# A decoder block's expert rows: scattered by slot, or gathered tile by tile through an inverted token map

## The chip, the cores and the metric

One core of a Trainium2 chip runs the whole program in one launch. The metric is the device time of one execution in microseconds (us), taken as the median of several runs.

## What is computed

The reference is one pre-norm decoder layer on 2048 tokens of width 512, in float32: self attention, cross attention, and a mixture of 16 experts plus a shared one. The last part is what matters here:

```python
scores = softmax(xt @ Wg.T)                      # 2048 x 16
group_scores = scores.reshape(T, 4, 4).max(-1)   # the best 2 of 4 groups stay
topi = top_k(masked, 4)[1]                       # 4 experts of each token
h = silu(einsum('td,eid->eti', xt, W1)) * einsum('td,eid->eti', xt, W3)
y = einsum('etd,te->td', einsum('eti,edi->etd', h, W2), combine)
z = silu(xt @ Ws1.T) * (xt @ Ws3.T) @ Ws2.T      # shared expert, 704 wide
x = x + y + z
```

`xt` is the layer-normed row of each token. The kernel computes an expert only for the tokens that chose it.

## The kernel before

The program runs in stages: self attention, cross attention, then `route_and_share` (layer norm, router, and the first half of the shared expert), `routed_experts`, and `combine_and_share` (the second half of the shared expert, and the sum of each token's four results). Rows are kept as pairs of float16, a high and a low part, so a token's row is 2 x 512 values, 2 KB.

**Slots.** 2048 tokens with 4 experts each give 8192 slots in 64 tiles of 128, and since each expert's slots begin at a new tile, up to `TILES` = 84 tiles exist in DRAM (`slot_rows`, 10752 rows of 2 KB); the number that holds tokens is known only at run time, and the loop over tile pairs stops there. Rows of a tile that belong to no token must hold finite values, so self attention's SP clears all of `slot_rows` with 12 transfers (L773), three in each of four groups.

**Routing.** In `route_and_share`, VectorE (DVE) turns the router's 16 score columns into ranks, choices and, with two products of TensorE (PE) against triangular and full matrices of ones (L1569), into places. L1648 writes `fx_index`: 128 x 64 slot numbers, one for each of the 16 token tiles and 4 choices. Then GpSimd (POOL) issues 64 indirect transfers (L1555), four abreast, each of which writes 128 rows of `fx_rows` from SBUF to their slots in DRAM. Meanwhile DVE computes the weights of the choices (`ro_hit`, L1656 to L1658).

**The shared expert.** `SharedExpert.tensor` is PE's part: four rounds of 512 tokens. `hidden(g)` is 72 products (L78 is the line of the helper) into `sh_ab`, `outputs(g)` 36 products into `sh_yp`. ScalarE (ACT) applies Silu and writes the high part, DVE (for the first three POOL) multiplies and makes the low part (L1453, L1459), and DVE adds the results to `x_sb` (L1464). hidden(0) comes first, then the two products for places; then a loop does hidden(g+1) and outputs(g).

**Routed experts.** SP reads `slot_rows` with transposing transfers into `re_xt` (L1732), two tiles ahead of PE, each as soon as PE has used the buffer. PE does 36 products per tile into `re_ab`, turns the hidden rows (L1809), and does the outputs `re_yp` of a tile behind the hidden products of the next one. POOL keeps the weights: two experts' are in SBUF as pairs; for each further expert e it waits for the last output of expert e-2 (`y_done`), casts the raw weights to the high part (L1765), makes the low part in 16 shares (L1769) and starts the four raw loads of expert e+2 between them (L1749). Results go to `slot_outs` by ACT's queue. Combine gathers them by `fx_index` (L1918).

## Time and profile before

| what | value |
|---|---|
| runs | 1793.79, 1798.22, 1806.79 us; median 1798.22 |
| profiled execution | 1793.67 us, span 1791.9 us |
| TensorE busy | 1477.0 us, 82% of the span |
| mean granted TensorE clock | 0.916 |
| shared expert 0, beside the scatters | about 1042 to 1200 us of the span |
| routed experts | about 1201 to 1678 us |
| combine and shared expert 1 | 1678 us to the end |

Every time in a row of the trace is counted from the span's start; the profiled execution as a whole took 1.8 us more than its span. "Busy" is time in which an engine executes; the releaser behind an arrow is what ended the idle time before a row, and "issue" is idle time for which the profile shows no releaser.

### The profile page before, as it was taken

The page shows a single profiled execution, that of the slowest core. Times are in us where ns is not written, and L with a number is a line of the kernel's source. Part 1 is how long each engine was busy: PE and PEld are TensorE (multiplying, and loading weights), DVE is VectorE, ACT ScalarE, POOL GpSimd, SP SyncE. Part 2 cuts the span into 40 slices and gives each one's busy share as a digit, 9 for nine tenths or more (in the row PEclk, how much of TensorE's full clock was granted, in tenths as well). Part 3 has the DMA queues.
Part 4 walks back from the last instruction along what each step waited for, and adds up shares of the span by engine and source line. Part 5 has one row for each costly group of instructions (what it writes and reads, how often), then busy time and mean ns, then how long its engine had stood idle before and what let it go on. Part 6 is the DMA issues. An engine that isn't in the chain of part 4 may idle for free. (4 is left out here: it accounts for less than half of the span.)

```text
span 1791.9 us, 28528 instructions
## 1 busy us (share of the span) xinstructions
PE 1477.0 (82%) x9520; PEld 694.0 (39%) x9521; DVE 1072.2 (60%) x1851; ACT 621.5 (35%) x1107; POOL 655.4 (37%) x675
## 2 busy tenths in 40 slices
PE   4689999864788888888888595287999999999988
PEld 2355545431222222222222352044555555556443
DVE  6446465567788888888986562022454444444476
ACT  4242404131465665665667540011111111111121
POOL 1000001134633333333201237502664646657374
PEclk9899999895688999999999788598999999999999
DMA  5862538214711311311200125407655566663465
GB/s 210 247 183 89 156 116 237 79 57 87 221 40 35 69 30 42 72 31 30 60 1 1 52 118 205 152 12 157 185 157 162 161 162 150 173 182 87 121 200 186
DMA packets 197159, 211.25 MB, mean 118 GB/s; under 512 B 90000, under 2 KB 162256, under 8 KB 196688
## 3 DMA queue, kind: packets, MB, share of 16 engines
q1 hardware_dynamic: 167696, 123.67, 26.5%
q0 software_dynamic: 18592, 66.99, 12.2%
q10 hardware_dynamic: 10784, 19.47, 2.9%
q8 instruction: 50, 0.82, 0.2%
q14 instruction: 37, 0.30, 0.1%
HBM read 101.09 MB, written 88.87 MB: 106 GB/s over the span
## 5 line engine op out<-in xcount | busy, mean ns | idle before, releaser
L1040 DVE TENSOR_REDUCE ca_mx<-ca_sc 128x1 f32<-128x512 f32 x512 | 327.5, 676 | 81.5 <-PE ca_sc L948 81.0
L78 PE MATMUL re_ab<-fx_w,re_xt 128*128 x1800 | 297.0, 315 | 18.3 <-DMA re_xt<-slot_rows 18.3
L1190 ACT ACTIVATE ca_pt<-ca_st 128x512 f32<-128x512 f32 x512 | 264.7, 596 | 102.7 <-PE ca_st L960 102.7
L948 PE MATMUL ca_sc<-ca_ks,ca_qs 48*128 48x512 f16 x512 | 186.8, 418 | 56.5 <-DVE ca_mx L1040 31.6
L78 PEld LDWEIGHTS re_ab<-fx_w,re_xt 128*128 128x128 f16 x1800 | 173.9, 98 | 116.8 <-issue 21.0
L960 PE MATMUL ca_st<-ca_qs,ca_ks 49*128 49x512 f16 x512 | 171.5, 399 | 42.1 <-ACT ca_pt L1190 36.5
L78 PE MATMUL sh_ab<-fx_xn,sh_pair 128*128 (+3 forms) x576 | 137.6, 398 | 35.5 <-issue 31.7
L78 PE MATMUL re_yp<-fx_w,re_ht 128*128 (+1 forms) x666 | 156.0, 379 | 0.0
L1769 POOL TENSOR_TENSOR fx_w<-re_raw_w,fx_w 128x272 f16<-128x272 f32 x224 | 153.9, 723 | 1.7
L973 PE MATMUL ca_pv<-ca_pt,ca_va 128*32 128x512 f32 x1024 | 149.3, 647 | 1.0 <-DVE ca_turned L1053 0.5
L960 PEld LDWEIGHTS ca_st<-ca_qs,ca_ks 49*128 49x128 f16 x512 | 42.0, 95 | 237.5 <-ACT ca_pt L1190 152.3
L1850 ACT ACTIVATE re_gate<-re_ab 128x352 f32<-128x352 f32 x75 | 34.7, 463 | 255.6 <-PE re_ab L78 197.5
L1765 POOL CAST fx_w<-re_raw_w 128x4352 f16<-128x4352 f32 x14 | 53.3, 3808 | 158.1 <-PE re_yp L78 158.1
L756 POOL TENSOR_TENSOR sa_yt<-sa_yf,sa_yt 128x512 f16<-128x512 f32 x16 | 18.5, 1156 | 250.5 <-ACT sa_yt L690 250.5
L1243 POOL TENSOR_TENSOR ca_tf<-ca_tf,home 128x512 f32<-128x512 f32 x32 | 40.6, 1269 | 176.6 <-DVE ca_rf L1031 176.6
L78 PEld LDWEIGHTS sh_ab<-fx_xn,sh_pair 128*128 128x128 f16 (+1 forms) x576 | 63.1, 110 | 107.3 <-issue 49.1
L1877 DVE TENSOR_TENSOR re_hp<-re_hf,re_hp 128x352 f16<-128x352 f32 x75 | 78.2, 1042 | 42.1 <-ACT re_hp L1852 42.1
L1875 DVE TENSOR_TENSOR re_hf<-re_ab,re_gate 128x352 f32<-128x352 f32 x75 | 39.3, 524 | 105.5 <-PE re_ab L78 105.5
L1886 DVE COPY re_ht<-re_ht_ps 128x768 f16<-128x768 f16 x74 | 41.2, 557 | 101.0 <-PE re_ht_ps L1809 100.9
L1252 POOL TENSOR_TENSOR ca_yt<-ca_yf,ca_yt 128x512 f16<-128x512 f32 x32 | 37.0, 1156 | 170.4 <-ACT ca_yt L1179 170.4
L78 PE MATMUL sa_proj<-sa_xn,sa_w 128*128 128x512 f16 x384 | 89.8, 388 | 5.0 <-DVE home L579 3.9
L1918 POOL DMA_INDIRECT co_yg<-slot_outs,fx_index x64 | 73.4, 1147 | 54.5 <-POOLq L1697 28.6
(242 smaller groups left out, 2343.3 us busy)
## 6 DMA issues: line engine op xcount, KB each, us to landing
re_raw_w<-in_we POOLq DMA_DIRECT2D x56, 544.0 KB, 4.6
slot_rows<-sa_zeros SPq DMA_DIRECT2D x12, 1792.0 KB, 16.0
slot_outs<-re_ys ACTq DMA_DIRECT2D x74, 256.0 KB, 2.0
sa_scratch<-home SPq DMA_DIRECT2D x16, 512.0 KB, 3.7
ca_scratch<-ca_qk SPq DMA_DIRECT2D x64, 128.0 KB, 1.8
sa_qs<-sa_scratch SPq DMA_DIRECT2D x12, 512.0 KB, 6.8
sa_ks<-sa_scratch SPq DMA_DIRECT2D x12, 512.0 KB, 6.6
ca_qs<-ca_scratch SPq DMA_DIRECT2D x48, 128.0 KB, 3.7
```

The costliest lines, as they stand in the source:

```text
L78: last = nc.tensor.matmul(out, lhs(a, c), rhs(b, c), start=(m == 0), stop=(m == total - 1), skip_group_check=parts > 1)
L948: nc.tensor.matmul(sc[:, m % RING, :], qs[rows, c % SLOTS, pair, qt * P:(qt + 1) * P], ks[rows, c % SLOTS, pair, :], start=True, stop=True ...
L960: nc.tensor.matmul(st[:, m % RING, :], ks[rows, b % SLOTS, pair, kt * P:(kt + 1) * P], qs[rows, b % SLOTS, pair, :], start=True, stop=True ...
L973: last = nc.tensor.matmul(pv[j * 32:(j + 1) * 32, :], va[:, b % 2, kt, h, :], pt[:, (4 * qd + j) % 8, :], start=(kt == 0), stop=(kt == 3), ...
L1040: nc.vector.reduce_max(mx[:, qd // 4, qd % 4, 2 * a + jj:2 * a + jj + 1], sc[:, m % RING, :], AX.X).then_inc(maxed, 1)
L1190: nc.scalar.activation(pt[:, (4 * qd + k) % 8, :], st[:, m % RING, :], ACT.Exp, scale=SCALE).then_inc(exp_done, 1)
L1243: nc.gpsimd.tensor_tensor(tf[:, u, :], tf[:, u, :], freq[:, 0, :], ALU.mult).then_inc(rolled, 1)
L1765: nc.gpsimd.tensor_copy(w[:, e % 2, 0, :], raw_w[:, e % 2, :]).then_inc(w_high, 1)
L1769: nc.gpsimd.tensor_tensor(w[:, e % 2, 1, at], raw_w[:, e % 2, at], w[:, e % 2, 0, at], ALU.subtract).then_inc(w_low, 1)
L1877: nc.vector.tensor_tensor(hp[:, s, 1, :], hf[:, s, :], hp[:, s, 0, :], ALU.subtract).then_inc(h_low, 1)
L1886: nc.vector.tensor_copy(ht[:, s, :, :], ht_ps[:, 0:2 * IC, :]).then_inc(ht_ready, 1)
L1918: nc.gpsimd.indirect_dma_start(out=yg[:, m % RING, :], out_offset=None, in_=slot_outs, in_offset=bass.IndirectOffsetOnAxis(ap=route["index ...
```

## The change

The rows are written to DRAM in token order, and each slot tile is gathered from there.

1. `layer_norm`'s SP stores the 16 tiles of token rows in a new DRAM tensor `token_rows`. The 12 clears of `slot_rows` are gone.
2. DVE splits `fx_index` into tile number (`high`) and row in the tile (`low`), and builds, in four chunks of 16 choices, two one-hot matrices in the freed `fx_rows`: `at_tile` (one operation of 128 x 1344 a chunk) and `at_row`, times the token's number (16 operations of 128 x 128 a chunk). Three products and low parts of the shared expert stand between the chunks. The computation of the weights and the adds of the first round come behind it.
3. PE multiplies them, 64 products of 84 columns summed in one bank, behind hidden(1), which is moved ahead of the loop; DVE casts the sum to `fx_tokens`, 128 x 84: which token's row stands in each slot. A slot without a token gets row 0.
4. POOL gathers the first 40 tiles (`AHEAD`) by it into a ring of 6 in SBUF, four in flight; SP stores each to `slot_rows`, two in flight, and transposes tiles 0 and 1 on the way.
5. The other 44 tiles are gathered and stored by POOL among the routed experts (`both`), in groups of 14, 7, 7, 7 and 9, each ahead of POOL's wait for `y_done` of experts 0 to 4. SP's transposes now also wait for `available`.
6. Combine's first four semaphores are those of the gathers.

```diff
 SPARE = TILES - T * TOPK // P
-assert CT * CLEARS * T // G == TILES and SPARE % (T // G) == 0
+assert SPARE % (T // G) == 0
+AHEAD = 40
...
+        @block.sync
+        def _(sp):
+            for t in range(NT):
+                sp.wait_ge(low_ready, t + 1)
+                sp.dma_start(token_rows[t * P:(t + 1) * P, :], pair(t).rearrange("p h d -> p (h d)")
+                             ).then_inc(rows_stored, 16)
...
-                    at = (g * CLEARS + k) * CT * P
-                    zero(slot_rows[at:at + CT * P], zeros[:, :])
                 share = SPARE // NG
...
@@ -1424,9 +1426,12 @@
 
         hidden(0)
         behind_first()
-        with pe.Fori(0, self.ROUNDS - 1) as g:
-            hidden(g + 1)
-            outputs(g)
+        hidden(1)
+        behind_second()
+        outputs(0)
+        with pe.Fori(0, self.ROUNDS - 2) as g:
+            hidden(g + 2)
+            outputs(g + 1)
         outputs(self.ROUNDS - 1)
...
+class Gathers:
...
+    def fetch(self, pool, m):
+        if m >= self.LANES:
+            pool.wait_ge(self.fetched[m % self.LANES], 16 * (m // self.LANES))
+        if m >= self.RING:
+            pool.wait_ge(self.landed[m % 2], 16 * ((m - self.RING) // 2 + 1))
+        self.start(m)
+
+    def start(self, m):
+        self.nc.gpsimd.indirect_dma_start(
+            out=self.staged[:, m % self.RING, :], out_offset=None, in_=self.token_rows,
+            in_offset=bass.IndirectOffsetOnAxis(ap=self.tokens[:, m:m + 1], axis=0)
+        ).then_inc(self.fetched[m % self.LANES], 16)
+    def store(self, engine, m, lanes, first=0):
+        engine.wait_ge(self.fetched[m % self.LANES], 16 * (m // self.LANES + 1))
+        if m >= first + 2:
+            engine.wait_ge(lanes[m % 2], 16 * ((m - first) // 2))
+        engine.dma_start(self.slot_rows[m * P:(m + 1) * P, :], self.staged[:, m % self.RING, :]).then_inc(lanes[m % 2], 16)
+
+    def take_over(self, pool):
+
+        for lane in self.landed:
+            pool.wait_ge(lane, 16 * AHEAD // 2)
+        pool.sem_inc(self.available, AHEAD)
+
+    def both(self, pool, first, count):
+
+        def store(m):
+            self.store(pool, m, self.landed_late, AHEAD)
+            if m >= AHEAD + 2:
+                pool.sem_inc(self.available, 1)
+
+        for m in range(first, count):
+            if m >= first + 3:
+                store(m - 3)
+            pool.wait_ge(self.fetched[m % self.LANES], 16 * (m // self.LANES))
+            if m >= AHEAD + self.RING:
+                pool.wait_ge(self.landed_late[m % 2], 16 * ((m - self.RING - AHEAD) // 2 + 1))
+            self.start(m)
+        for m in range(max(first, count - 3), count):
+            store(m)
+        if count == TILES and first < count:
+            for lane in self.landed_late:
+                pool.wait_ge(lane, 16 * (TILES - AHEAD) // 2)
+            pool.sem_inc(self.available, 2)
+
...
+        at_tile = flat_rows[:, 0:NT * TOPK * TILES].rearrange("p (n k) -> p n k", k=TILES)
+        at_row = flat_rows[:, NT * TOPK * TILES:NT * TOPK * (TILES + P)].rearrange("p (n k) -> p n k", k=P)
...
+            for m in range(AHEAD):
+                gathers.store(sp, m, gathers.landed)
+                if m in (4, 5):
+                    s = m - 4
+                    sp.wait_ge(gathers.landed[s], 16 * 2)
+                    sp.dma_start_transpose(xt[:, s, :, :], gathers.slot_rows[s * P:(s + 1) * P, :]).then_inc(x_loaded[s], 16)
...
-            pool.wait_ge(milestones, ROUTED)
-            for m, (t, k) in enumerate(sends):
-                if m >= ABREAST:
...
+            pool.wait_ge(rows_stored, 16 * NT)
+            pool.wait_ge(milestones, INVERTED)
+            for m in range(AHEAD):
+                gathers.fetch(pool, m)
...
+            def invert():
+
+                share = NT * TOPK // CHUNKS
+                for n in range(NT * TOPK):
+                    if n % share == 0:
+                        pe.wait_ge(milestones, PLACED + n // share + 1)
+                    last = nc.tensor.matmul(tokens_at, at_row[:, n, :], at_tile[:, n, :], start=(n == 0),
+                                            stop=(n == NT * TOPK - 1))
+                last.then_inc(placed, 1)
+
+            shared.tensor(pe, places_and_totals, invert)
...
+            index = route["index"][:, :, :].rearrange("p t k -> p (t k)")
+            link(nc.vector.tensor_scalar(high_i[:, :], index, 7, None, ALU.arith_shift_right))
+            step(nc.vector.tensor_scalar(low_i[:, :], index, P - 1, None, ALU.bitwise_and))
+            link(nc.vector.tensor_copy(high[:, :], high_i[:, :]))
+            step(nc.vector.tensor_copy(low[:, :], low_i[:, :]))
+            dve.wait_ge(rows_stored, 16 * NT)
+            share = NT * TOPK // CHUNKS
+            for c in range(CHUNKS):
+                n0 = c * share
+                nc.vector.tensor_tensor(
+                    at_tile[:, n0:n0 + share, :],
+                    steps[:, 0:TILES].rearrange("p (o k) -> p o k", o=1).to_broadcast([P, share, TILES]),
+                    high[:, n0:n0 + share].rearrange("p (n o) -> p n o", o=1).to_broadcast([P, share, TILES]), ALU.is_equal)
+                for n in range(n0, n0 + share):
+                    last = nc.vector.tensor_scalar(at_row[:, n, :], steps[:, :], low[:, n:n + 1],
+                                                   token[:, n // TOPK:n // TOPK + 1], ALU.is_equal, ALU.mult)
+                last.then_inc(milestones, 1)
+                if c == 0:
+                    shared.wait_low(dve, shared.by_pool - 1)
+                if c < IC:
+                    shared.product(dve, nc.vector, IC + c)
+                    shared.low_part(dve, nc.vector, IC + c)
+            dve.wait_ge(placed, 2)
+            nc.vector.tensor_copy(route["tokens"][:, :], tokens_at).then_inc(milestones, 1)
+            for t in range(4):
+                shared.add(dve, x_sb, t)
+            step(nc.vector.memset(hit[:, :, :], 0.0))
             for k in range(TOPK):
-                if k < IC:
-                    shared.product(dve, nc.vector, IC + k)
                 tk = top[:, :, k:k + 1].to_broadcast([P, NT, E])
...
-            for t in range(4):
-                shared.add(dve, x_sb, t)
...
-            for s in range(2):
-                turn_rows(s, s)
             n = turns(sp)
             with sp.Fori(0, n) as i:
                 for s in range(2):
 
                     sp.wait_ge(ab_done, 2 * i + s + 1)
-                    sp.sem_inc(slot_free, 1)
+                    sp.sem_inc(freed, 1)
+                    sp.wait_ge(gathers.available, 2 * i + s + 3)
+                    sp.sem_inc(freed, 1)
                     turn_rows(s, 2 * i + 2 + s)
...
+            fetched_by = [AHEAD, AHEAD + 14, AHEAD + 21, AHEAD + 28, AHEAD + 35] + [TILES] * (E - 4)
+            gathers.take_over(pool)
...
             for e in range(2, E):
+                gathers.both(pool, fetched_by[e - 2], fetched_by[e - 1])
                 done = pool.value_load(route["ends"][0:1, e - 2:e - 1], min_val=0, max_val=TILES)
                 pool.wait_ge(y_done, done + 2)
-                pool.sem_inc(w_free, 1)
+                pool.sem_inc(freed, 1)
```

What stands on PE between hidden(0) and the loop over the rounds (`sh_ab` are the hidden products, `sh_yp` the outputs). Before:

```order
L78 MATMUL sh_ab<-fx_xn,sh_pair 96x512 x24
L1569 MATMUL ro_spots<-ro_chosen,ro_earlier 128x256
L1569 MATMUL ro_spots<-ro_chosen,ro_every 128x256
L1427 UNCONDITIONAL_BRANCH
L1427 ISA
```

and after the change:

```order
L1647 MATMUL ro_spots<-ro_chosen,ro_earlier 128x256
L1647 MATMUL ro_spots<-ro_chosen,ro_every 128x256
L77 MATMUL sh_ab<-fx_xn,sh_pair 128x512 x48
L77 MATMUL sh_ab<-fx_xn,sh_pair 96x512 x24
L1657 MATMUL ro_spots<-fx_rows 128x84 x64
L77 MATMUL sh_yp<-sh_pair,sh_ht 128x512 x36
L1432 UNCONDITIONAL_BRANCH
```

hidden(1) and outputs(0) have left the loop, and the 64 products of the inversion stand between them.

On POOL, from the scatters to the wait ahead of expert 2's cast. Before:

```order
L1555 DMA slot_rows<-fx_rows,fx_index 10752x1024 x64
L1474 UNCONDITIONAL_BRANCH
L1745 UNCONDITIONAL_BRANCH
L1749 DMA re_raw_w<-in_we 128x1088 x8
L1761 TENSOR_LOAD fx_ends
```

and after (ten further pairs of L1503 and L1494 stand at the dots):

```order
L1494 DMA ga_staged<-token_rows,fx_tokens 128x1024 x40
L1537 UNCONDITIONAL_BRANCH
L1850 UNCONDITIONAL_BRANCH
L1854 DMA re_raw_w<-in_we 128x1088 x8
L1494 DMA ga_staged<-token_rows,fx_tokens 128x1024 x3
L1503 DMA slot_rows<-ga_staged 128x1024
L1494 DMA ga_staged<-token_rows,fx_tokens 128x1024
...
L1503 DMA slot_rows<-ga_staged 128x1024 x3
L1870 TENSOR_LOAD fx_ends
```

Gathers and stores of 14 tiles have come between the raw loads and the wait.

On DVE, behind the index; `sh_hf` and `sh_ht` are the shared expert's product and low part, `ro_hit` the weights' working tile. Before:

```order
L1648 TENSOR_SCALAR fx_index<-ro_top 128x64
L1649 MEMSET ro_hit 128x256
L1453 TENSOR_TENSOR sh_hf<-sh_gate,sh_lin 128x512
L1656 TENSOR_TENSOR ro_hit<-ro_slot,ro_top 128x256
L1657 TENSOR_TENSOR ro_hit<-ro_hit,ro_s 128x256
```

and after (one chunk of four):

```order
L1737 TENSOR_SCALAR fx_index<-ro_top 128x64
L1739 TENSOR_SCALAR ro_high_i<-fx_index 128x64
L1740 TENSOR_SCALAR ro_low_i<-fx_index 128x64
L1741 CAST ro_high<-ro_high_i 128x64
L1742 CAST ro_low<-ro_low_i 128x64
L1747 TENSOR_TENSOR fx_rows<-ro_steps,ro_high 128x1344
L1752 TENSOR_SCALAR fx_rows<-ro_steps,ro_low,ro_token 128x128 x16
L1458 TENSOR_TENSOR sh_hf<-sh_gate,sh_lin 128x512
L1464 TENSOR_TENSOR sh_ht<-sh_hf,sh_ht 128x512
```

A chunk of one-hot rows has come ahead of each product, and the weights have gone behind the chunks.

## Rows read from the trace of the kernel before

**Rows 1.** The page's part 1: busy us, share of the span, instructions.

```profile
PE 1477.0 (82%) x9520; PEld 694.0 (39%) x9521; DVE 1072.2 (60%) x1851; ACT 621.5 (35%) x1107; POOL 655.4 (37%) x675
```

**Rows 2.** The table by windows: start:end, length, each engine's busy time, granted clock, DMA share.

```profile
core 0: us, PE busy (x) PEld busy (x) DVE busy (x) ACT busy (x) POOL busy (x), PEclk, DMA share, GB/s
1068.00:1095.00 27.00, 24.97 (x117) 11.75 (x115) 16.08 (x32) 4.05 (x7) 20.75 (x19) 1.00 0.46 175
1095.00:1158.00 63.00, 17.19 (x35) 4.76 (x32) 1.38 (x2) 1.72 (x3) 43.20 (x45) 0.57 0.50 191
1158.00:1201.00 43.00, 39.45 (x173) 17.53 (x173) 14.93 (x22) 8.45 (x15) 0.00 (x0) 0.95 0.00 0
1250.00:1678.00 428.00, 410.43 (x2713) 246.28 (x2710) 198.54 (x284) 66.89 (x140) 249.97 (x320) 1.00 0.56 153
1678.00:1792.00 114.00, 99.65 (x432) 45.60 (x432) 73.60 (x104) 20.46 (x36) 73.44 (x64) 0.93 0.62 184
```

**Rows 3.** POOL's groups from 1040 us on: count, busy us, mean ns, idle before by releaser.

```profile
L1918 POOL DMA_INDIRECT co_yg<-slot_outs,fx_index x64 | 73.4, 1147 | 54.5 <-POOLq L1697 28.6 <-issue 15.9 <-DVE x_sb L1938 10.1
L1555 POOL DMA_INDIRECT slot_rows<-fx_rows,fx_index x64 | 63.9, 999 | 23.3 <-issue 19.2 <-DVE ro_hit L1649 4.1
```

**Rows 4.** The timeline of PE in the shared stage: start, us, instruction, idle before.

```profile
1085.16 10.09 PE L78 MATMUL sh_ab<-fx_xn,sh_pair 128*128 x46
...
1124.48 0.58 PE L78 MATMUL sh_ab<-fx_xn,sh_pair 128*96 x1 [2.22 <-issue]
```

**Rows 5.** The timeline of PE at full pace, and its first routed products.

```profile
1059.64 15.70 PE L78 MATMUL sh_ab<-fx_xn,sh_pair 128*128 x72
...
1183.83 15.97 PE L78 MATMUL sh_yp<-sh_pair,sh_ht 128*128 128x512 f16 x72
1204.63 8.03 PE L78 MATMUL re_ab<-fx_w,re_xt 128*128 x36 [4.83 <-DMA re_xt<-slot_rows]
```

**Rows 6.** The timelines of SP's queue and of PE at the clears.

```profile
61.14 11.65 SPq L773 DMA_DIRECT2D slot_rows<-sa_zeros  x3
...
68.90 0.60 PE L466 MATMUL sa_sc<-sa_ks,sa_qs 96*128 96x128 f16 x4 [14.32 <-DMA sa_ks<-sa_scratch]
```

**Rows 7.** The timelines of DVE around the index and of PE at the router.

```profile
1066.23 1.32 DVE L1646 MAX8 ro_top<-ro_slot 128x8 f32<-128x16 f32 x16
1067.58 0.20 DVE L1648 TENSOR_SCALAR fx_index<-ro_top 128x64 int32<-128x64 f32 x1
...
1068.26 0.69 DVE L1453 TENSOR_TENSOR sh_hf<-sh_gate,sh_lin 128x512 f32<-128x512 f32 x1
...
1070.23 0.69 DVE L1459 TENSOR_TENSOR sh_ht<-sh_hf,sh_ht 128x512 f16<-128x512 f32 x1
...
1087.26 1.55 DVE L1665 TENSOR_TENSOR ro_passed<-ro_tile_no,ro_ends 1x1344 f32<-1x1344 f32 x1
...
1039.64 1.16 PE L78 MATMUL ro_spots<-ro_wg,fx_xn 128*128 128x16 f16 x36
```

**Rows 8.** The timeline of POOL in the routed experts.

```profile
1211.18 2.18 POOL L1749 DMA_DIRECT2D re_raw_w<-in_we  x4 [59.57 <-PE re_ab L78]
...
1221.45 1.56 POOL L1749 DMA_DIRECT2D re_raw_w<-in_we  x3 [0.22 <-issue]
1248.06 3.81 POOL L1765 CAST fx_w<-re_raw_w 128x4352 f16<-128x4352 f32 x1 [25.05 <-PE re_yp L78]
...
1272.69 3.80 POOL L1765 CAST fx_w<-re_raw_w 128x4352 f16<-128x4352 f32 x1 [6.36 <-PE re_yp L78]
...
1297.31 3.81 POOL L1765 CAST fx_w<-re_raw_w 128x4352 f16<-128x4352 f32 x1 [6.36 <-PE re_yp L78]
...
1388.79 3.81 POOL L1765 CAST fx_w<-re_raw_w 128x4352 f16<-128x4352 f32 x1 [12.22 <-PE re_yp L78]
```

**Rows 9.** The page's DMA issues, and the landing times of re_xt's transposes.

```profile
slot_outs<-re_ys ACTq DMA_DIRECT2D x74, 256.0 KB, 2.0
...
DMA to landing us min/median/max: 3.0/3.3/18.2
```

More of the change, by code:

```diff
@@ L1474, in route_and_share @@
+def route_and_share(nc, split, sems, ident, x_sb, moments, xn, rows, route, wg_dram, we_dram, token_rows, gathers, first_pairs,
+                    xt, x_loaded):
     with ExitStack() as ctx:
@@ L1518, in route_and_share @@
         hit = sb("hit", [P, NT, E], F32)
+        high_i = sb("high_i", [P, NT * TOPK], I32)
+        low_i = sb("low_i", [P, NT * TOPK], I32)
+        high = sb("high", [P, NT * TOPK], F16)
+        low = sb("low", [P, NT * TOPK], F32)
+        steps32 = sb("steps32", [P, P], F32)
+        steps = sb("steps", [P, P], F16)
+        token = sb("token", [P, NT], F32)
         tile_no = sb("tile_no", [1, TILES], F32)
-        passed = sb("passed", [1, TILES, E], F32)
+        end = NT * TOPK * (TILES + P)
+        passed = flat_rows[0:1, end:end + 2 * TILES * E].bitcast(F32).rearrange("o (t e) -> o t e", e=E)
         owner = sb("owner", [1, TILES], F32)
@@ L1545, in _ @@
                                     base=0, pattern=[[1, P]], channel_multiplier=-1).then_inc(made, 1)
-            sends = [(t, k) for t in range(NT) for k in range(TOPK)]
             for n in range(shared.by_pool):
@@ L1907, in combine_and_share @@
         yg = sb("yg", [P, RING, D], F32)
-        fetched = [sem(f"fetched{r}") for r in range(RING)]
-        used, ready, stored = sem("used"), sem("ready"), sem("stored")
+        fetched = gathers.fetched + [sem(f"fetched{r}") for r in range(gathers.LANES, RING)]
+        earlier = [16 * TILES // gathers.LANES] * gathers.LANES + [0] * (RING - gathers.LANES)
+        used, stored = sem("used"), sem("stored")
         fetches = [(t, k) for t in range(NT) for k in range(TOPK)]
```

86 lines of the change are left out of this document (43 added, 43 removed).

## The prediction, made before the changed kernel was run

> **What bounds the kernel now.** First the page: PE is busy for 1477.0 of 1791.9 us, POOL for 655.4 [rows 1], so PE is the engine to follow, and the question is where it isn't busy. The table by windows answers it [rows 2]: in the shared expert's stage PE has 24.97 of 27 us, then only 17.19 of 63, then 39.45 of 43. The stretch of 63 us is the one hole that the change touches directly. What fills it is seen twice. POOL's groups show the 64 scatters, 0.999 us each, 63.9 in all, with 19.2 us of "issue" between them [rows 3]: 1.30 from start to start. They can begin when the index is ready, at 1067.8, and so last until 1151, and the last one's data lands a few us later. The timeline of PE shows that it waits for no semaphore there: 46 matmuls run in 10.09 us up to 1095, then they come one by one, eleven of them, as the one shown, with 2.22 us of "issue" before it [rows 4]. It is over by 1158, as the scatters are. Nothing in the trace names the cause; it is slow instruction supply that begins 27 us into the scatters. At full pace the hidden part of a round is 72 matmuls in 15.70 us, its outputs 36, half of the 15.97 that 72 take: 8.0 [rows 5]. PE ends the stage at 1199.8, and the first routed product runs at 1204.63, at half clock, for which it waited 4.83 us.
>
> **Clears.** The 12 clears go, three of four issued at 61.14 in 11.65 us. One wait of PE for sa_ks ends behind them, 14.32 us [rows 6]; most of it is the load's own path. Between 0 and 3 us; I take -2.
>
> **Tokens.** The index is written at 1067.58 + 0.20. Four small DVE operations on 64 columns (0.20 each) follow: 1068.7. Then four chunks: one comparison over 1344 columns, 1.55 by the row of the same size, and 16 one-hot rows of 128 columns. Such rows are not in the trace: one over 64 columns takes 0.20 and the 16 MAX8 over 8 start 0.08 apart; I take 0.17 (0.10 to 0.25) and a chunk of 1.5 + 2.7 = 4.2, together 16.8. Between the chunks stand three pairs of product and low part, from 1068.26 to 1070.23 + 0.1 apart with ACT's part between: 2.1 each, 6.3. Sum 1091.8. The last 16 matmuls of 84 columns, by the router's 36 of 16 columns in 1.16 with more columns, about 1.6, the cast and semaphores 0.4 [rows 7]: tokens near 1094 (1088 to 1102). PE meanwhile ends the second hidden part, at 1059.64 + 15.70 = 1075.3 [rows 5], and then has only the 64 matmuls until 1093.7; this wait of 18 us is new, and outputs(0) and everything of PE stand behind it.
>
> **PE's shared stage.** What is left is outputs(0), two rounds of hidden and outputs, outputs(3): 8.0 + 15.7 + 8.0 + 15.7 + 16.0 = 63.4, and 3 for a clock that falls to half in the new wait (before, 0.57 was granted in the hole) [rows 2]: 1160, where it was 1199.8. This takes for granted that the slow supply is gone with the scatters; rival A denies it.
>
> **Gathers.** POOL starts 40 from 1094.3. The nearest rows are co_yg's, also 256 KB by an index: 73.4 busy and 15.9 of issue for 64, 1.40 from start to start [rows 3]. But here each tile's bytes cross the DMA engines twice, in and out by SP, so I take 1.6 (1.30, the scatters' pace, to 2.3): 39 x 1.6 + 6 for the landings of gather and store = 1162.7 (1150 to 1190). Routed starts near 1164. Its first two transposes have been done, so the wait of 4.83 before re_ab goes: first product 1164.1, -40.5. POOL's first raw load then comes at 1168.2 (the first tile runs at full clock; before 6.55 behind the first product, now 4.1), and its second batch, which ends at 1221.45 + 1.56 before, at 1180.0, -43.
>
> **In the experts.** Here the gain is partly given back, and this is the term that decides. POOL's next work before was the cast for expert 2, waiting 25.05 us for PE, then 6.36, then 12.2 in each of the following [rows 8]. Cast and low parts and loads of one expert take 24.63 - 6.36 = 18.3. An expert of four tiles lasts 24.6, one of five 30.5, a tile so 6.1. POOL now has gathers and stores ahead of each of the waits: 14, 7, 7, 7 and 9 tiles. One costs a gather, 1.15 + 0.2, and a store, 0.544 by the raw load's row + 0.16, together 2.05; a group ends with a wait of about 0.5 for its last gather, the fifth with 3 for its last stores. So 29.2 + 3 x 14.9 + 21.5 = 95.4. POOL is then never idle: 1180.0 + 95.4 + 5 x 18.3 = 1366.9 for expert 6's weights, with PE waiting for weights from expert 3 on. Expert 5's last outputs follow one tile later, 1373.0, where it was 1388.79: -15.8. Queued behind POOL's waits are the raw loads of the next expert, and behind these the casts; that is in the sum. From there POOL has no extra work, 18.3 against 30.5, and PE sets the end as before. Of some 40 us won, 25 are given back.
>
> The bound of this price from below: the gathers alone at 1.3 to 1.4, the stores hidden, where POOL's sum falls to 60 and PE's own pace sets the end: at best -43. From above: stores with a whole landing of a 256 KB transfer, 2.0 [rows 9], half of it beside POOL's next gather, 3.0 a tile. I take 2.05, nearest to the rows of issue, since three tiles are in flight.
>
> The longest landing of a transpose before is 18.2 against a median of 3.3 [rows 9], beside the eight raw loads; two tiles of PE cover 12.2. The Trainium skill, "DMA: Bandwidth & Descriptors", section "Queues, rings and completion order", says that each DMA engine takes turns between its queues packet by packet. By that rule a transpose's small packets each wait for one large packet of POOL's queue, and its landing grows several times, wherever POOL moves rows; the slow row agrees in sign. If the landings stay under 12.2 the sum stays as it is. At the slow row's 18.2 each tile so hit would cost the excess, 6.0; seven such tiles would bring the 42 us of rival B by another way, and its chance holds this too.
>
> **Other edits.** The 16 stores of token rows lie in the layer norm, on SP, ahead of the routing. Weights and adds moved behind the tokens: the adds are wanted only from outputs(0), which now comes later itself. PE's loop over rounds is a round shorter and starts a round later in both shared experts; the order of the matmuls in the second one stays but for hidden(1) ahead of outputs(0), as before. Combine's semaphores: nothing. The last stage, 99.65 of 114 [rows 2], is untouched.
>
> **Sum.** 1793.7 (the profiled execution) - 15.8 - 2 = 1775.9. The median of the runs, 1798.2, stands 4.5 above that execution, the lowest 0.1; I add 2: 1778.
>
> **Rivals.**
>
> A, the slow supply stays. For it: its cause is unknown, DRAM is written by rows in both kernels, and 80 transfers are under way. Against it: no such phase shows beside clears or the 64 gathers of the last stage. If it comes 27 us into the gathers, at 1121, PE has 36 us of work left, does about 12% of its full pace (by 35 matmuls in 63 us, at 0.22 each) to 1160 and ends at 1195. POOL is free at 1212, and 1212 + 95.4 + 91.5 + 6.1 = 1405: +16.4 - 2, so 1810.
>
> B, the other side: POOL's share in the experts costs 3.0 a tile, because each store waits for the landing two before it while the DMA engines are shared with loads and transposes. 44 x 0.95 = 42 more than the forecast: 1820. It decides from 2.5 us a tile; over 1% slower from 2.9. For it: the DMA engines are 0.56 busy in the experts' stretch as it is [rows 2], and each tile adds 512 KB to read, stage and write. Against it: the lanes leave three tiles in flight.
>
> C, POOL's share is cheap, near 1.4 a tile: PE sets the pace at once, and nearly all of the 43 stays: 1755.
>
> That the change doesn't do what it says, which is to free PE of the hole, is A as well.
>
> **Chances.** Forecast 0.50, A 0.26, B 0.12, C 0.12. A measurement tells about 1%, here 18 us, from no change: faster is under 1780.2, slower above 1816.2. The forecast's own range is 1765 to 1792, so 0.29 of its 0.50 is faster; with C 0.41. A is 0.16 within and 0.10 slower, B 0.10 slower and 0.02 within. Faster 0.41, same 0.39, slower 0.20. The range runs from C to B, 1754 to 1824.
>
> **What would show it.** Right: tokens cast near 1094; PE with no "issue" rows between 1094 and 1160; the fortieth gather near 1157; re_ab first near 1164; POOL without idle time before the casts of experts 3 to 6, PE waiting for POOL there, some 5 us an expert; the cast of expert 7 near 1373. Wrong: "issue" before single matmuls again (A); stores L1503 with a wait for their own lane, or re_ab waiting for DMA in experts 1 to 6 (B); the cast for expert 7 before 1360 (C). A one-hot row above 0.3 us would shift everything by 8 us or more.

## The result, and the profile after the change

| | kernel before | changed kernel |
|---|---|---|
| median of runs | 1799.41 us (1793.79 to 1806.79, 4 runs) | 1845.59 us (1843.13 to 1855.03, 4 runs) |
| ratio | | 1.027, 95% interval 1.0211 to 1.0328 |
| span of the profiled execution | 1791.9 us | 1841.3 us |
| mean granted clock | 0.916 | 0.902 |

The change makes the kernel 2.7% slower. The forecast was 1778 with a range up to 1824; it was wrong in sign and in range.

The page's first part, and the two groups of it that speak of the change (busy, mean ns, idle before), against [rows 1]:

```profile
PE 1482.8 (81%) x9568; PEld 701.2 (38%) x9585; DVE 1077.8 (59%) x1925; ACT 621.8 (34%) x1107; POOL 696.8 (38%) x741
...
L77 PE MATMUL re_ab<-fx_w,fx_xt 128*128 x1800 | 302.6, 319 | 107.1 <-POOLq L1884 74.3
...
L1494 POOL DMA_INDIRECT ga_staged<-token_rows,fx_tokens x84 | 83.0, 988 | 86.9 <-DMA slot_rows<-ga_staged 34.5
```

PE has hardly more work than before, 1482.8 against 1477.0. But the routed experts' hidden products (`re_ab`) now have 107.1 us of idle time in all before them, 74.3 of it until POOL, at L1884, raised `w_ready` for an expert's weights; before, the same products had waited 18.3 us in all, for transposes. The gathers waited 34.5 us for stores to land. The table by windows, against [rows 2]:

```profile
core 0: us, PE busy (x) PEld busy (x) DVE busy (x) ACT busy (x) POOL busy (x), PEclk, DMA share, GB/s
1068.00:1095.00 27.00, 11.20 (x87) 7.04 (x86) 24.70 (x78) 3.83 (x7) 0.00 (x0) 0.73 0.00 1
1095.00:1158.00 63.00, 62.86 (x297) 29.70 (x298) 28.16 (x50) 10.16 (x18) 29.50 (x29) 0.98 0.83 229
1158.00:1201.00 43.00, 14.84 (x83) 8.18 (x82) 5.00 (x9) 1.92 (x4) 12.63 (x15) 0.68 0.70 223
1250.00:1400.00 150.00, 105.30 (x657) 62.02 (x658) 48.13 (x66) 15.83 (x33) 107.58 (x139) 0.85 0.75 206
```

The hole of 63 us is gone: PE has 62.86 of 63 where it had 17.19. In its place PE has 11.20 of 27 ahead of it, 14.84 of 43 behind it, and 105.30 of 150 in the experts. Note the column before the last, the DMA engines' share: 0.83, 0.70 and 0.75 in the last three windows. The timeline of PE in the shared stage:

```profile
1096.01 8.77 PE L77 MATMUL sh_yp<-sh_pair,sh_ht 128*128 128x512 f16 x36
...
1143.72 15.97 PE L77 MATMUL sh_yp<-sh_pair,sh_ht 128*128 128x512 f16 x72
1186.52 7.15 PE L77 MATMUL re_ab<-fx_w,fx_xt 128*128 x36 [26.82 <-issue]
```

PE ends the stage at 1159.7, as the forecast said (1160), and then stands still for 26.82 us. The profile names no releaser there; the code does. The stage ends for all engines together, so PE stays until SP and POOL have started all 40 gathers and stores, and in the next stage POOL raises `w_ready` for the first two experts only behind `take_over`, which waits until the 40 stores have landed. PE's first product needs only tile 0, and SP had started the transposes of tiles 0 and 1 by 1115. No run tries the stage with a smaller `AHEAD` or with the weights released earlier. The timeline of POOL, through the gathers and what comes after:

```profile
1097.39 1.13 POOL L1494 DMA_INDIRECT ga_staged<-token_rows,fx_tokens  x1 [32.79 <-DVE fx_tokens L1761]
...
1177.06 0.95 POOL L1494 DMA_INDIRECT ga_staged<-token_rows,fx_tokens  x1 [1.23 <-DMA slot_rows<-ga_staged]
...
1202.09 2.10 POOL L1854 DMA_DIRECT2D re_raw_w<-in_we  x4 [7.70 <-DMA re_raw_w<-in_we]
1204.49 1.01 POOL L1494 DMA_INDIRECT ga_staged<-token_rows,fx_tokens  x1 [0.30 <-issue]
...
1213.44 0.59 POOL L1503 DMA_DIRECT2D slot_rows<-ga_staged  x1 [5.40 <-DMA ga_staged<-token_rows,fx_tokens]
...
1233.50 0.58 POOL L1503 DMA_DIRECT2D slot_rows<-ga_staged  x1 [2.50 <-DMA slot_rows<-ga_staged]
...
1245.71 0.54 POOL L1503 DMA_DIRECT2D slot_rows<-ga_staged  x1 [2.26 <-DMA slot_rows<-ga_staged]
1246.84 3.81 POOL L1874 CAST fx_w<-re_raw_w 128x4352 f16<-128x4352 f32 x1 [0.59 <-issue]
...
1285.75 3.81 POOL L1874 CAST fx_w<-re_raw_w 128x4352 f16<-128x4352 f32 x1 [0.32 <-issue]
...
1412.63 4.11 POOL L1874 CAST fx_w<-re_raw_w 128x4352 f16<-128x4352 f32 x1 [2.67 <-DMA slot_rows<-ga_staged]
...
1442.21 3.81 POOL L1874 CAST fx_w<-re_raw_w 128x4352 f16<-128x4352 f32 x1 [8.92 <-PE re_yp L77]
```

The 40 gathers take from 1097.39 to 1177.06, 2.04 us from start to start. Then come POOL's 14 later tiles, from the end of its raw loads at 1204.19 to the cast at 1246.84, and so on: the rows show the pattern of gather, wait, store, and the casts of experts 2, 3, 6 and 7. Before, the cast of expert 7 stood at 1388.79 [rows 8]; it stands at 1442.21. That is +53.4, of which 4.0 come back up to the end.

### The profile page after: what moved, and what is told of

Read it like the earlier page. It is cut to its first block and busy times, and to the rows that moved or that the text cites. A ratio compares the mean times of both kernels' runs of the same rounds, so it can differ in the third digit from the quotient of the medians.

```text
span 1841.3 us, 29056 instructions
## 1 busy us (share of the span) xinstructions
PE 1482.8 (81%) x9568; PEld 701.2 (38%) x9585; DVE 1077.8 (59%) x1925; ACT 621.8 (34%) x1107; POOL 696.8 (38%) x741
## 5 line engine op out<-in xcount | busy, mean ns | idle before, releaser
L77 PE MATMUL re_ab<-fx_w,fx_xt 128*128 x1800 | 302.6, 319 | 107.1 <-POOLq L1884 74.3
L77 PEld LDWEIGHTS re_ab<-fx_w,fx_xt 128*128 128x128 f16 x1800 | 175.5, 100 | 210.6 <-issue 114.7
L950 PE MATMUL ca_sc<-ca_ks,ca_qs 48*128 48x512 f16 x512 | 188.0, 422 | 53.2 <-DVE ca_mx L1042 30.5
L77 PE MATMUL sh_ab<-fx_xn,sh_pair 128*128 128x512 f16 (+3 forms) x576 | 129.1, 387 | 3.8 <-PEq L1804 3.3
L1494 POOL DMA_INDIRECT ga_staged<-token_rows,fx_tokens x84 | 83.0, 988 | 86.9 <-DMA slot_rows<-ga_staged 34.5
L1961 ACT ACTIVATE re_hp<-re_hf 128x352 f16<-128x352 f32 x75 | 37.2, 496 | 169.3 <-DVE re_hf L1984 164.7
L77 PEld LDWEIGHTS re_yp<-fx_w,re_ht 128*128 128x128 f16 (+1 forms) x666 | 65.1, 98 | 69.9 <-issue 1.1
```

The source lines that it names most:

```text
L77: last = nc.tensor.matmul(out, lhs(a, c), rhs(b, c), start=(m == 0), stop=(m == total - 1), skip_group_check=parts > 1)
L950: nc.tensor.matmul(sc[:, m % RING, :], qs[rows, c % SLOTS, pair, qt * P:(qt + 1) * P], ks[rows, c % SLOTS, pair, :], start=True, stop=True ...
L1494: self.nc.gpsimd.indirect_dma_start(out=self.staged[:, m % self.RING, :], out_offset=None, in_=self.token_rows, in_offset=bass.IndirectOff ...
```

## The experiments

The profiled executions differ by up to 9 us in where the shared stage's second hidden part begins (1059.6 to 1068.7), whatever the kernel, so a place in that stage is compared with the first scatter or gather of its own execution.

**What makes the hole?** Runs on the kernel before. "Hole" is the stretch in which PE's matmuls come one by one with "issue" before them [rows 4].

`b_plain`:

```diff
-                nc.gpsimd.indirect_dma_start(
-                    out=slot_rows, out_offset=bass.IndirectOffsetOnAxis(ap=route["index"][:, t, k:k + 1], axis=0),
-                    in_=rows[:, t, :, :].rearrange("p h d -> p (h d)"), in_offset=None
-                ).then_inc(sent[m % ABREAST], 16)
+                pool.dma_start(slot_rows[m * P:(m + 1) * P, :], rows[:, t, :, :].rearrange("p h d -> p (h d)")
+                               ).then_inc(sent[m % ABREAST], 16)
```

> The kernel before, with each of its 64 indirect scatters replaced by a plain store of the same 256 KB from SBUF to slot_rows, same engine, same four abreast. It leaves the routing of rows out. Theory S (the slow supply of PE's instructions comes with the indirect writes of rows, whose targets lie scattered in DRAM): the hole goes, PE issues without gaps, the stage ends near 1151 instead of 1199.8, total near 1747. Rival W (any 17 MB written to DRAM at this rate does it): the hole stays, total near 1794. Rival L (it is the code of the loop over rounds): stays too.

Measured: 1731.22, beside 1801.92 for the kernel before on that chip. PE issues without gaps and ends the stage at 1148.8. The same bytes to DRAM do nothing to PE, so W falls. Nor is it a matter of busy DMA engines: their share was 0.89 here from 1082 to 1125 us, beside a PE that has no "issue" at all, and 0.50 in the hole [rows 2]. The total is 16 us below what S gave; 11.6 of these lie in the experts, where five tiles took 29.3 us instead of 30.5 [rows 8], and this is not explained (see the end).

`b_half`:

```diff
-            sends = [(t, k) for t in range(NT) for k in range(TOPK)]
+            sends = [(t, k) for t in range(NT) for k in range(TOPK // 2)]
```

> The kernel before with only the first 32 of the 64 scatters; half of the rows aren't moved. S and W: the single-file matmuls begin about 27 us into the scatters as before and end as the 32nd scatter lands, about 42 us after the first, so the hole is about 17 us long instead of 63 and the total near 1757. L: the hole stays as long as it is, total near 1794.

Measured: 1755.7, as S and W gave. The gaps begin near 1104, 27 us behind the first scatter, and end at 1123, with the scatters. The hole lasts as long as the scatters do.

`b_order`:

```diff
-        with pe.Fori(0, self.ROUNDS - 1) as g:
-            hidden(g + 1)
-            outputs(g)
+        hidden(1)
+        outputs(0)
+        with pe.Fori(0, self.ROUNDS - 2) as g:
+            hidden(g + 2)
+            outputs(g + 1)
```

> The kernel before with only PE's order changed as in the changed kernel: hidden(1) and outputs(0) written out ahead of the loop over rounds. S and W: the hole stays (it begins when the scatters are 27 us old, whatever code runs), total within 8 us of 1794. L: the hole moves or goes, total down by up to 45 us.

Measured: 1802.97, and the hole is there from 1100 to 1163. L falls: the order of PE's code, which the change also alters, has no part in it. A run that was to put 10 to 25 us ahead of the first scatter gave no result.

`b_abreast2`, and the same timed as `b_abreast2_t`, and `b_abreast3`:

```diff
-ABREAST = 4
+ABREAST = 2
```

(With 3, which doesn't divide 64, the last wait also takes each semaphore's own count.)

> The kernel before with two scatters in flight instead of four. S and W, if it is the number in flight that starves the fetch: scatters 2 us or more apart, PE free of gaps, routed stage from about 1068 + 64 x 2 = 1200 on, total near 1792. If it is the writes as such: gaps as long as the scatters last, about 1200, and a total of 1810 to 1830. L: no change of the hole.

> The kernel before with two scatters in flight, timed: the one run of it was 1760.3 against 1801.9. The same again: 1756 to 1764, a ratio near 0.98.

> The kernel before with three scatters in flight. If three are few enough for the instruction supply: scatters 1.3 us apart instead of 1.5, the routed stage starts 12 us earlier than with two, total near 1748. If they aren't: the hole is back, total 1790 to 1800.

Measured: with two in flight 1760.31 in the first run, where no theory had put it (1792, or 1810 to 1830): PE is free of gaps, but the scatters come 1.52 us apart and not the 2 or more expected. In the median of four it is 1768.74, a ratio of 0.985 (0.9793 to 0.9904), above the 1756 to 1764 expected from the first run. With three 1796.41, 0.9985 (0.9941 to 1.0029), and the hole is back. What differs is told by POOL's groups in one line each (count, busy, mean ns, idle before by releaser); two in flight:

```profile
L1555 POOL DMA_INDIRECT slot_rows<-fx_rows,fx_index x64 | 64.1, 1002 | 36.7 <-DMA slot_rows<-fx_rows,fx_index 31.4 <-DVE ro_hit L1649 4.1 <-issue 1.2
```

three in flight:

```profile
L1555 POOL DMA_INDIRECT slot_rows<-fx_rows,fx_index x64 | 64.3, 1004 | 23.2 <-issue 19.2 <-DVE ro_hit L1649 4.1
```

With two, 59 of the scatters were preceded by a wait for a landing, of 0.53 us on average. With three there was none: the 0.3 us of "issue" before each are the same as with four [rows 3]. So three act like four, and what two bring is a wait before nearly each scatter. A new theory (Q below) says: PE's instructions are held back while POOL issues indirect transfers with no pause between.

**What do the later tiles cost the experts?** Three runs on the changed kernel; a fourth asks what the clears cost.

`a_fit`:

```diff
-            fetched_by = [AHEAD, AHEAD + 14, AHEAD + 21, AHEAD + 28, AHEAD + 35] + [TILES] * (E - 4)
+            fetched_by = [AHEAD + n for n in (0, 8, 10, 12, 16, 20, 24, 28, 32, 36, 40, 42, 44, 44, 44)]
```

> The changed kernel with the 44 later tiles in other groups ahead of the same waits of POOL: 8, 2, 2, 4, 4, 4, 4, 4, 4, 4, 2, 2 instead of 14, 7, 7, 7, 9, so that at some 3 us a tile each group fits into the idle time that POOL has ahead of that cast in the kernel before (25, 6, 6, then 12 us). The order is enough for this routing, in which no expert owns more than five tiles. Theory P (POOL's time ahead of the casts is what the experts lose by): no cast is late any more, the experts run at the pace of before from the first routed product at 1186.5 on, total 1186.5 + 587 = 1774 (1766 to 1780). Rival D (the DMA engines' load delays transposes and raw loads wherever it lies): PE keeps waiting for re_xt or for weights, total above 1810.

Measured: 1811.72, beside 1795.01 for the kernel before: 34 less than the changed kernel's median, but 38 more than P gave. It also lies just above the 1810 from which D was to hold. POOL still goes from work to work. The timeline of one group of four, ahead of expert 6's cast:

```profile
1340.47 1.03 POOL L1494 DMA_INDIRECT ga_staged<-token_rows,fx_tokens  x1 [0.30 <-issue]
...
1346.48 0.58 POOL L1503 DMA_DIRECT2D slot_rows<-ga_staged  x1 [2.45 <-DMA ga_staged<-token_rows,fx_tokens]
...
1352.86 0.54 POOL L1503 DMA_DIRECT2D slot_rows<-ga_staged  x1 [2.05 <-DMA slot_rows<-ga_staged]
1353.71 3.81 POOL L1873 CAST fx_w<-re_raw_w 128x4352 f16<-128x4352 f32 x1 [0.31 <-issue]
```

From the first gather to the cast these four tiles take 13.2 us, not 12.2: each group first waits for its first gather (2.45) and at its end for landings (2.05 before the last store), so a small group costs more per tile: one of two tiles took 8.6 us (26.9 from cast to cast, less 18.3). Other groups of four took up to 15.7 us (34.0 from cast to cast, less 18.3). So P's statement that no cast would be late is wrong. Its mechanism fits the waits of PE's `re_ab` all the same: 33.3 us for late weights, where the changed kernel had 74.3, and 5.8 for transposes, where it had 5.7, so what is left of the loss is still POOL's time. D speaks of waits for weights too, and this total doesn't part the two; `a_thin` does more. The version isn't faster than the kernel before.

`a_thin` (the clears are put back so that the tiles hold numbers):

```diff
     def start(self, m):
+        if m >= AHEAD:
+            self.nc.gpsimd.indirect_dma_start(
+                out=self.staged[0:16, m % self.RING, :], out_offset=None, in_=self.token_rows,
+                in_offset=bass.IndirectOffsetOnAxis(ap=self.tokens[0:16, m:m + 1], axis=0)
+            ).then_inc(self.fetched[m % self.LANES], 16)
+            return
...
-        engine.dma_start(self.slot_rows[m * P:(m + 1) * P, :], self.staged[:, m % self.RING, :]).then_inc(lanes[m % 2], 16)
+        n = P if m < AHEAD else 16
+        engine.dma_start(self.slot_rows[m * P:m * P + n, :], self.staged[0:n, m % self.RING, :]).then_inc(lanes[m % 2], 16)
```

> The changed kernel with 16 of 128 rows gathered and stored in each of the 44 later tiles, so that 1/8 of the bytes moves there with the same instructions; most rows of these tiles aren't moved (slot_rows is cleared ahead, as before the change). Theory B (the 3.05 us a tile are the DMA engines' time for 512 KB beside loads and transposes): a tile falls to POOL's issue time, 1.9, the groups from 134 to 84 us, total near 1793. Rival F (it is the fixed latency of landings with two stores in flight): a tile stays at 2.7 or more, total above 1825.

Measured: 1810.03. B gave 1793, F more than 1825. Three of its rows, the second raw loads, and the casts of experts 2 and 3:

```profile
1205.87 2.09 POOL L1866 DMA_DIRECT2D re_raw_w<-in_we  x4 [7.59 <-DMA re_raw_w<-in_we]
...
1239.14 3.81 POOL L1886 CAST fx_w<-re_raw_w 128x4352 f16<-128x4352 f32 x1 [0.66 <-issue]
...
1272.18 3.81 POOL L1886 CAST fx_w<-re_raw_w 128x4352 f16<-128x4352 f32 x1 [0.40 <-PE re_yp L79]
```

From the end of the loads (1207.96) to the cast the 14 tiles take 31.2 us, 2.2 each; the next seven take 33.04 - 18.3 = 14.7, 2.1 each. The changed kernel took 42.7 and 20.6 for the same. All five groups together took 96.6 us, where the changed kernel had 135.3 and the forecast 95.4. What POOL waited for before its later stores shows where the difference lies (total, times, longest); changed kernel, 1204 to 1413 us:

```profile
POOL slot_rows L1503 <- DMA slot_rows<-ga_staged: 36.7, 21, 2.9
...
POOL slot_rows L1503 <- DMA ga_staged<-token_rows,fx_tokens: 10.9, 5, 5.4
```

and `a_thin`, 1204 to 1380 us:

```profile
POOL slot_rows L1515 <- DMA ga_staged<-token_rows,fx_tokens: 7.7, 4, 4.7
...
POOL slot_rows L1515 <- DMA slot_rows<-ga_staged: 6.0, 6, 1.3
```

This is B: with the bytes gone a tile costs nearly what its instructions cost, and the wait for earlier stores falls from 36.7 us to 6.0. A thin tile has 1/8 of the rows as well as of the bytes; no run tells the two apart. The total lies 17 above my number because I had worked it out with 1.9, and because at 2.2 POOL's work still isn't hidden: PE waited 34.4 us for late weights.

`a_lanes`: four semaphores for the stores of SP and four for those of POOL, each store waiting for the fourth before it.

```diff
-    RING, LANES = 6, 4
+    RING, LANES, EARLY, LATE = 6, 4, 4, 4
...
-        if m >= first + 2:
-            engine.wait_ge(lanes[m % 2], 16 * ((m - first) // 2))
+        s = len(lanes)
+        if m >= first + s:
+            engine.wait_ge(lanes[(m - first) % s], 16 * ((m - first) // s))
...
```

> The changed kernel with four stores in flight instead of two, in both places. B: no or little gain, since the engines are full: the shared stage's gathers stay 2.0 us apart, total within 8 us of the changed kernel's 1843. F: the gathers of the shared stage come 1.4 to 1.6 us apart (-18 us) and a tile in the experts costs 2.3 (-30 us), total near 1797.

Measured: 1853.99, 11 above the 1843 of B, which had allowed 8, and 57 above what F gave. The windows of its gathers in the shared stage and of its first later group:

```profile
1105.00:1172.00 67.00, 59.43 (x274) 27.55 (x272) 28.39 (x49) 10.16 (x18) 37.06 (x37) 0.97 0.93 288
1210.00:1240.00 30.00, 23.85 (x148) 14.09 (x149) 7.46 (x13) 3.35 (x7) 18.24 (x24) 0.89 1.08 258
```

and the same two places of the changed kernel:

```profile
1104.00:1178.00 74.00, 55.55 (x256) 25.81 (x254) 27.00 (x47) 10.16 (x18) 34.83 (x35) 0.90 0.89 255
1213.00:1246.00 33.00, 23.63 (x156) 14.13 (x156) 9.20 (x16) 3.84 (x8) 18.57 (x25) 0.98 1.01 278
```

The DMA engines were 0.89 and 1.01 busy with two stores in flight, 0.93 and 1.08 with four (the table's shares can come out a little over 1). The shared stage's gathers came 1.83 us apart instead of 2.04, which is 8 us, so they didn't "stay 2.0 us apart", as B had it, either. In the experts nothing was won: PE waited 61.7 us for weights and 18.1 for transposes, together 79.8, where the changed kernel had 74.3 and 5.7. F falls.

`a_clears` (the wait for the clears is put back too):

```diff
+                for k in range(CLEARS):
+                    at = (g * CLEARS + k) * CT * P
+                    zero(slot_rows[at:at + CT * P], zeros[:, :])
```

> The changed kernel with the 12 clears of slot_rows put back. If their removal was worth something: 2 to 3 us slower than the changed kernel, with the difference in the first 200 us. If they were hidden: the first 200 us equal, total within 1 us (one run can't tell more than that from the total; the windows can).

Measured: 1846.59, 1.0 above the changed kernel's median. From 60 to 100 us, in the changed kernel:

```profile
60.00:100.00 40.00, 30.61 (x176) 16.59 (x180) 18.27 (x36) 7.59 (x10) 4.48 (x4) 0.83 0.29 73
```

and with the clears:

```profile
60.00:100.00 40.00, 30.28 (x174) 16.34 (x178) 18.37 (x35) 7.33 (x10) 4.48 (x4) 0.83 0.68 211
```

The DMA engines do 0.29 or 0.68, PE 30.61 or 30.28: hidden. PE's wait for `sa_ks` ends at 68.86 without the clears and at 69.19 with them; before it was 68.90 [rows 6].

**Back to the hole, and the forecast's sum.**

`a_allthin`: as `a_thin`, but for all 84 tiles.

> The changed kernel with 16 of 128 rows gathered and stored in each of all 84 tiles: 1/8 of the bytes, all instructions; most rows aren't moved. If the bytes' time in the DMA engines is all that the forecast mis-sized, it now comes out: gathers of the shared stage 1.3 to 1.6 us apart, the routed stage from 1164 on, a tile in the experts 2.1, total 1774 to 1790. If something else is missing as well, it stays above 1800.

Measured: 1816.2. Neither: the hole came back, in a kernel that scatters nothing. PE in it, and behind the dots POOL's gathers at the same time:

```profile
1112.58 0.38 PE L79 MATMUL sh_ab<-fx_xn,sh_pair 128*128 x1 [0.72 <-issue]
...
1118.21 0.59 PE L79 MATMUL sh_ab<-fx_xn,sh_pair 128*128 x1 [2.40 <-issue]
...
1123.92 5.79 PE L79 MATMUL sh_ab<-fx_xn,sh_pair 128*128 x12 [0.81 <-issue]
1136.26 3.69 PE L79 MATMUL sh_ab<-fx_xn,sh_pair 128*96 x9 [6.55 <-issue]
...
1114.92 0.84 POOL L1500 DMA_INDIRECT ga_staged<-token_rows,fx_tokens  x1 [0.30 <-issue]
1117.66 0.83 POOL L1500 DMA_INDIRECT ga_staged<-token_rows,fx_tokens  x1 [1.90 <-DMA slot_rows<-ga_staged]
1120.49 0.96 POOL L1500 DMA_INDIRECT ga_staged<-token_rows,fx_tokens  x1 [2.00 <-DMA slot_rows<-ga_staged]
...
1126.78 0.84 POOL L1500 DMA_INDIRECT ga_staged<-token_rows,fx_tokens  x1 [0.30 <-DMA slot_rows<-ga_staged]
```

PE's gaps begin at 1112, after 12 gathers without a wait. At 1117.66 and 1120.49 POOL waits 1.90 and 2.00 us for stores, and from 1120 on PE runs again; in the next 18 gathers, which have no such wait, it stands again (6.55 before 1136.26). S falls with this too: these gathers read, and move 32 KB each. What they have in common with the scatters is POOL's unbroken row of indirect transfers, and its pace, 1.14 us from start to start here. The bytes' part can still be read: 40 gathers took 1098.23 to 1153.39, 1.41 from start to start, against 2.04.

Two more kernels from the kernel before, `b_pause16` and `b_pause8`:

```diff
                 if m >= ABREAST:
                     pool.wait_ge(sent[m % ABREAST], 16 * (m // ABREAST))
+                if m and m % 16 == 0:
+                    pool.wait_ge(sent[(m - 1) % ABREAST], 16 * ((m - 1) // ABREAST + 1))
```

> The kernel before, four scatters in flight, with a wait for the landing of the scatter just issued ahead of every 16th. Theory Q (PE's instruction supply is held back while POOL issues indirect transfers without a pause, and a pause of a few us lets it catch up): no run of scatters is longer than 16, or 20 us, and the hole began after 21 of them, 27 us; no hole or short gaps, scatters done near 1162, total 1745 to 1760. Rival N (it is four in flight, or the writes as such): the hole stays but for the three pauses, total 1780 to 1800.

> The same with the wait ahead of every 8th. Q: no hole at all, seven pauses of some 3 us, scatters done near 1172, total 1755 to 1765. N: gaps between the pauses, total above 1775.

Measured: every 16th 1770.46, ratio 0.9837 (0.9812 to 0.9862); every 8th 1768.6, 0.9825 (0.9792 to 0.9858). The totals decide nothing: the first lies between Q's 1760 and N's 1780, the second above Q's 1765 and below N's 1775. PE's rows do. The sum of what PE waited for from 1090 to 1730 us, by releaser (total, times, longest), in the kernel before:

```profile
PE sh_ab L78 <- issue: 31.7, 16, 5.8
...
PE sh_yp L78 <- issue: 14.9, 8, 2.9
```

with a pause every 16th:

```profile
PE sh_ab L78 <- issue: 10.5, 11, 3.7
PE sh_yp L78 <- issue: 10.3, 6, 3.2
```

and with one every 8th:

```profile
PE re_ab L78 <- DMA re_xt<-slot_rows: 43.1, 4, 38.2
...
PE sh_ab L78 <- issue: 2.7, 4, 1.7
```

Of 46.6 us of "issue" some 20 are left with 16, and 2.7 with 8. So N falls: with four in flight and the same writes, seven pauses of 2.5 us take the hole away. Now PE waits 38.2 us once, for the first transpose, because the scatters end late: the limit has gone to POOL.

Q in its own words doesn't hold, though. With a pause every 16th, PE's first gap is this one, and it begins at 1105, at the ninth scatter behind the first pause, after the first 16 in a row had passed without any:

```profile
1108.26 3.47 PE L78 MATMUL sh_yp<-sh_pair,sh_ht 128*128 128x512 f16 x9 [3.24 <-issue]
```

And in the last stage of the kernel before, POOL issues 24 gathers between 1697.22 and 1730.17 us with 0.3 us before each but the first, while PE has no "issue" in the whole stage and, in this row, its full pace:

```profile
1724.16 15.70 PE L78 MATMUL sh_ab<-fx_xn,sh_pair 128*128 x72
```

Those come 1.43 us apart; in the hole it is 1.27. By the mean from the first to the last transfer, the runs with a hole have 1.31 (kernel before, three in flight), 1.41 (`a_allthin`) and 1.42 (every 16th), those without 1.52 (two in flight), 1.54 (`a_thinpause`, below), 1.58 (every 8th) and 2.04 (changed kernel). So it may be the pace of the indirect transfers and not the missing pause that counts; no run parts the two, for every pause slows the pace as well.

`a_thinpause`: `a_allthin` with such a wait ahead of every 6th gather of the shared stage.

> The changed kernel with 1/8 of the bytes in all 84 tiles, as in the run before, and a wait for the landing of the gather just issued ahead of every 6th in the shared stage. Q: the single-file matmuls that this run had without the pauses go, PE ends the stage near 1160, and what the forecast took for the bytes is all that is left out of it: total 1776 to 1792. N, or something else still missing from the forecast: above 1800.

Measured: 1786.61, in the range that Q gave; the single-file matmuls are gone, and PE has one "issue" of 0.54 us left in the shared stage. This execution's shared stage began 8.5 us later than the changed kernel's (its second hidden part at 1068.71 against 1060.19). PE starts the experts at 1174.77, which is 1166.3 without that lag, against the forecast's 1164.1. The cast of expert 7:

```profile
1389.26 3.81 POOL L1888 CAST fx_w<-re_raw_w 128x4352 f16<-128x4352 f32 x1 [9.02 <-PE re_yp L79]
```

Without the lag it is 1380.8; the forecast had 1373.0, the changed kernel 1442.21.

## Why the prediction was wrong

The term that failed is the price of a later tile in the experts, 2.05 us, which measured 3.07; behind it comes the pace of the first 40 gathers, 1.6 us, which measured 2.04. Both were priced by POOL's instructions, and both are set by the rows that the DMA engines have to move. By its own steps, between the forecast's 1775.9 and the profiled 1843.1:

- **Clears** (-2): measured 0, since they were hidden. 2 us missed.
- **Tokens** (ready near 1094): the gathers began at 1097.4. The chunks were on time but for the one-hot rows, here the first 16:

```profile
1070.13 3.65 DVE L1752 TENSOR_SCALAR fx_rows<-ro_steps,ro_low,ro_token 128x128 f16<-128x128 f16 x16
```

  0.23 each instead of 0.17; the three pairs of product and low part cost 2.0 instead of 2.1. Late by 3.1 in all.
- **PE's shared stage** (1160): the number was right, 1159.7, in part by luck. PE began outputs(0) at 1096.0, 2.3 late, and the 3 us set aside for the clock were nearly all left over: 63.7 us for a sum of 63.4. And the forecast let the hole go "with the scatters". It went beside gathers that came 2.04 us apart, most of which waited for a store to land; where they come faster, rival A comes true, as `a_allthin` shows. At the forecast's own 1.6 no run was made.
- **Gathers** (1.6 us apart, taken from 1.30 to 2.3): measured 2.04, +17.3 over 39; with the later start and a longer landing at the end, the first routed product came at 1186.5 instead of 1164.1, +22.4. The reason was in the text, that the bytes cross twice, but only 0.2 us of it in the number. `a_allthin` gives 1.41 with 1/8 of the bytes.
- **In the experts** (2.05 a tile, 95.4 in all): the step that failed most. The five groups took 42.7, 20.6, 19.3, 21.6 and 31.1, together 135.3, or 3.07 a tile: +39.9. The forecast priced POOL's instructions, took them as nearest to the rows, and had the DMA engines' load, 0.56 [rows 2], only in rival B. `a_thin` shows that the instructions' price was right (96.6 us in all, 2.2 a tile) and that nearly 1 us a tile is the wait for the bytes; `a_lanes` that it isn't the number of stores in flight.
- The rest up to expert 7's cast was 7 us longer than the fixed 15.9, 18.3 and 6.1 of the sum, and from there on 4.0 were won that had not been forecast. 22.4 + 39.9 + 6.9 - 4.0 + 2.0 = 67.2, which is the whole difference.

Of the rivals, B had the mechanism (stores waiting for landings, on shared DMA engines) and its price, 3.0, within 0.1; of its two reasons the shared engines hold, and the wait for "the landing two before it" doesn't, by `a_lanes`. Its 1820 lacked the 22.4 us of the shared stage, 17.3 of which have the same cause. It was given 0.12. The range went wrong there too: its upper end, 1824, took the dear tiles and the slow gathers one at a time, though one cause drives both. The rule that was weighed, from the Trainium skill's page "DMA: Bandwidth & Descriptors", section "Queues, rings and completion order", that queues are served in turn packet by packet, would have the transposes fall behind beside POOL's rows. PE waited 5.7 us for them in all, against 18.3 before, so it cost nothing here that the runs show; but PE stood waiting for weights at the time, and a slower transpose could hide behind that. The changed kernel's profile gives no landing time for its transposes.

The sign follows: PE ends the shared stage 40.1 us earlier and waits 12.6 less for transposes, and it pays for that with 26.8 us of waiting for the gathers at the stage's end and 74.3 of waiting for weights. That leaves 48.4 us of the 49.4 by which the span grew. The end of the hole can be had for less: with two scatters in flight, or a pause every 16th or every 8th, and nothing else of the change, the kernel before runs at 0.985, 0.9837 and 0.9825 of its time. These three are the fastest versions of this study that do the whole computation. Their intervals overlap, so none of them is shown to be the best; each excludes 1, so each beats the kernel before, by under 2%.

## What to carry to other kernels

When a transfer is split in two steps, work its price out twice, once as the issuing engine's instructions and once as bytes over the DMA engines that are left free there, and take the larger. Here 153 GB/s stood in the experts' window [rows 2], and 512 KB every 2.05 us are 256 more, an estimate of 409 in all, where the windows above with the DMA engines 0.89 to 1.08 busy show 255 to 288. Work that is put ahead of an engine's wait costs nothing only up to that engine's idle time there, and groups pay for filling and draining each time. A stretch in which an engine waits for nothing the profile names deserves an experiment of one line before a redesign around it.

## What was new about the hardware

- PE's instructions came singly, mostly with 2.2 us before each, while POOL issued indirect transfers 1.27 us (scatters) or 1.14 us (small gathers) from start to start, with only 0.3 us between them; it began after 12 to 21 of them. Pauses of 2.5 us every 8th, or waits of 0.53 us before nearly each, prevent it; pauses every 16th don't wholly. 64 plain stores of the same bytes don't cause it. Nor do the last stage's gathers [rows 3], 24 of them in a row with 0.3 us between at 1.43 from start to start. That PE lacks its instructions there is only read from "issue", idle time for which the profile shows no releaser; which part of the chip is shared, and whether the pace or the missing pause counts, no run shows.
- An expert of five tiles takes 30.5 us in some executions and 29.3 in others (the kernel before, against the changed kernel behind expert 7 and `b_plain`); in the slower ones PE waits 1.0 us for `re_hp` once an expert. The trigger was not looked for.
